# A softmax maximum added by VectorE instead of by a rank-one matmul

## The reference, cut to what matters

```python
x = x + xattn(layernorm(x), ctx)      # 8 heads of 64: q = x@Wq, k = ctx@Wk, v = ctx@Wv
                                      # softmax(q k^T / 8) v, then @Wo + bo
x = x + attn(layernorm(x))            # one head of 512, causal mask, softmax
x = x + ffn(layernorm(x))             # 512 -> 2048 -> 512, relu, values rounded to fp8 and fp16
```

## Time and profile before

| | us |
|---|---|
| three runs | 1062.31, 1063.66, 1063.72 (median 1063.66) |
| the profiled execution | 1063.23, its span 1061.4 |
| TensorE busy | 1023.5 |
| VectorE, ScalarE, GpSimd busy | 517.4, 518.4, 412.7 |
| mean granted TensorE clock | 0.991 |

### The profile page before, as it was taken

How to read it: one execution, slowest core, us unless ns; L and a number is a source line. 1 busy time by engine, 2 the same in 40 slices (tenths; PEclk the granted TensorE clock), 3 DMA queues, 4 the chain that set the end, 5 groups by cost and what they waited for, 6 DMA issues and landing times.

```text
span 1061.4 us, 23899 instructions
## 1 busy us (share of the span) xinstructions
PE 1023.5 (96%) x10317; PEld 670.8 (63%) x10320; DVE 517.4 (49%) x864; ACT 518.4 (49%) x719; POOL 412.7 (39%) x230
## 2 busy tenths in 40 slices
PE   4899999999999999999999999999998899999998
PEld 2466767677776776767677676777766544554443
DVE  6454444444444444444444444446665463564533
ACT  3345655556655565655656555565554321222220
POOL 4235454444555444454454545443344651110000
PEclk9999999999999999999999999999999899999999
DMA  7221010001011110101011100101102101012302
GB/s 267 60 90 61 31 31 31 31 31 32 31 31 44 49 31 32 31 31 31 32 31 33 57 34 31 31 31 41 45 18 81 40 1 40 2 31 90 90 30 79
DMA packets 25462, 48.98 MB, mean 46 GB/s; under 512 B 2192, under 2 KB 2192, under 8 KB 25360
## 3 DMA queue, kind: packets, MB, share of 16 engines
q1 hardware_dynamic: 24784, 46.42, 13.5%
q10 hardware_dynamic: 576, 1.05, 0.3%
HBM read 45.36 MB, written 2.10 MB: 45 GB/s over the span
## 4 chain that ended last, share of the span: by engine, by line
PE 92%; DVE 4%; DMA 1%; issue 1%; ACT 1%; POOL 1%; SPq 0%; POOLq 0%
PE v_ps L360 25%; PE k_ps L360 24%; PE e_ps L426 8%; PE c_ps L360 8%; PE e_ps L360 6%; PE o_ps L444 6%; PE c_ps L399 4%; PE o_ps L446 3%; PE e_ps L419 3%; PE m_ps L617 1%; PE o_ps L617 1%; DMA wq_raw<-in_xwq 1%; PE k_ps L538 1%; PE v_ps L590 1%; DVE stats L1011 0%
## 5 line engine op out<-in xcount | busy, mean ns | idle before, releaser
L1198 POOL TENSOR_TENSOR p_l<-p_f,p_h 128x1024 f16<-128x1024 f32 x128 | 272.4, 2128 | 407.2 <-ACT p_f L745 407.2
L742 ACT ACTIVATE p_h<-e_ps 128x1024 f16<-128x1024 f32 x128 | 131.0, 1023 | 171.8 <-PE e_ps L426 171.8
L901 DVE TENSOR_TENSOR v<-v_ps,v 128x512 f16<-128x512 f32 x128 | 88.8, 694 | 257.6 <-ACT v L726 257.6
L914 DVE TENSOR_REDUCE part_max<-c_ps 128x2 f32<-128x1024 f32 x128 | 155.7, 1217 | 0.0
L909 DVE TENSOR_TENSOR k_l<-k_ps,k_h 128x512 f16<-128x512 f32 x128 | 88.5, 691 | 113.4 <-ACT k_h L734 113.4
L734 ACT ACTIVATE k_h<-k_ps 128x512 f16<-128x512 f32 x128 | 76.4, 597 | 130.5 <-PE k_ps L360 130.5
L745 ACT ACTIVATE p_f<-e_ps 128x1024 f32<-128x1024 f32 x128 | 130.4, 1019 | 0.0
L360 PE MATMUL v_ps<-wv_h,ctx_h 128*128 128x256 f16 x768 | 127.0, 274 | 1.4 <-DVE q_l L896 1.4
L360 PE MATMUL v_ps<-wv_l,ctx_h 128*128 128x256 f16 x768 | 125.7, 273 | 0.0
L360 PE MATMUL v_ps<-wv_h,ctx_l 128*128 128x256 f16 x768 | 125.7, 273 | 0.0
L444 PE MATMUL o_ps<-v,p_h 128*128 128x130 f16 x1024 | 106.9, 221 | 7.1 <-DVE o_all L939 3.7
(11 more groups left out here) (202 smaller groups left out, 1420.3 us busy)
## 6 DMA issues: line engine op xcount, KB each, us to landing
raw<-in_ctx_t SPq DMA_DIRECT2D x32, 768.0 KB, 4.5
w_raw<-in_w_t SPq DMA_DIRECT2D x32, 256.0 KB, 2.8
xr<-in_x SPq DMA_DIRECT2D x8, 256.0 KB, 5.3
out<-xr SPq DMA_DIRECT2D x8, 256.0 KB, 2.0
x_in<-in_x ACTq DMA_DIRECT2D x4, 256.0 KB, 5.5
x_in<-in_x SPq DMA_DIRECT2D x4, 256.0 KB, 5.2
wq_raw<-in_xwq SPq DMA_DIRECT2D x1, 1024.0 KB, 9.4
raw<-in_xwo SPq DMA_DIRECT2D x4, 256.0 KB, 3.3
```

Of the source, the lines that this page charges most:

```text
L742: act.activation(p_h[:, s % P_RING, :, :, :], scores, ACT.Exp, scale=EXP_SCALE, bias=SHIFT).then_inc(p_hi, 1)
L901: dve.tensor_tensor(v[g][:, j0:j0 + 2, :, DH + 1:2 * DH + 1], v_ps[:, :].rearrange("p (j h d) -> p j h d", j=2, d=DH), v[g][:, j0:j0 + 2, ...
L914: dve.tensor_reduce(part_max[:, s % QUARTERS, :], c_ps[:, :, :], AX, ALU.max).then_inc(c_maxed, 1)
L1198: pool.tensor_tensor(p_l[:, s % P_RING, :, :, :], p_f[:, s % F_RING, :, :, :], p_h[:, s % P_RING, :, :, :], ALU.subtract).then_inc(p_split, 1)
```

## The change

The rank-one products go. The maximum is spread once a stage: VectorE multiplies the identity by the negated maximum of each head (two 128x128 bf16 products, m_diag), TensorE multiplies a matrix of ones by m_diag (256 columns, in place of the transpose), and VectorE copies the result, the same in all partitions, to m_wide (f32, two buffers). In each slot a new VectorE operation, shift, adds e_ps and m_wide into p_f, first in its queue. ScalarE's two exponentials read p_f, the second in place. scores(s) no longer waits for the copied maximum, and waits for shifted instead of p_full. The setup of `pick` on GpSimd goes.

```diff
@@ -61,7 +61,7 @@
         ("bq_col", [P, DCH], F32), ("bk_col", [P, DCH], F32), ("b1_col", [P, HC, 1], F32),
         ("b2_half", [P, D], F16),
         ("stats", [P, B, 6], F32), ("mean_var", [P, B, 2], F32), ("rstd", [P, B], F32), ("exponent", [P, B], F32),
-        ("pick", [P, P], BF16), ("m_col", [P, 2, DH], F32), ("m_row", [P, 1, T], BF16),
+        ("ones", [P, P], BF16), ("m_col", [P, 2, 1], F32), ("m_diag", [P, 2, T], BF16), ("m_wide", [P, 2, 2, 1, T], F32),
         ("part_max", [P, QUARTERS, 2], F32), ("o_rec", [P, 2, 1], F32), ("o_low", [P, 2, DH], F32),
     ])
     queries, ctx0_base = place(nc, q_base, [("q_h", [P, PAIRS, B * T], F16), ("q_l", [P, PAIRS, B * T], F16)])
...
@@ -400,31 +402,28 @@
                                    start=True, stop=True)
                 mm.then_inc(c_filled, 1)
-            def turn_maximum(n):
-                pe.wait_ge(m_ready, n + 1)
+            def spread_maximum(n):
+                pe.wait_ge(diag_ready, n + 1)
                 if n:
                     pe.wait_ge(m_copied, n)
-                pe.transpose(m_ps[:, 0:T], m_col[:, :, :].rearrange("p h d -> p (h d)"), ident[:, :]).then_inc(m_turned, 1)
+                pe.matmul(m_ps[:, 0:2 * T], ones[:, :], m_diag[:, :, :].rearrange("p h i -> p (h i)"),
+                          start=True, stop=True).then_inc(m_spread, 1)
             def scores(s):
                 n, q = stage_of(s)
                 b, p = pair_of(n)
-                pe.wait_ge(m_copied, n + 1)
                 pe.wait_ge(k_split, s + 1)
                 if s:
-                    pe.wait_ge(p_full, s)
+                    pe.wait_ge(shifted, s)
                 tokens = slice(b * T, b * T + T)
-                for h, rows in enumerate(head_rows):
-                    pe.matmul(e_ps[:, h, :].rearrange("p (j i) -> p j i", j=JT), pick[rows, :],
-                              m_row[rows, :, :].broadcast_to([DH, JT, T]), start=True, stop=False)
                 for j in range(JT):
                     keys_at = slice(q * QW + j * P, q * QW + j * P + P)
                     last = j == JT - 1
-                    for left, right, stop in ((k_h, q_h, False), (k_h, q_l, False), (k_l, q_h, last)):
+                    for left, right, first, stop in ((k_h, q_h, j == 0, False), (k_h, q_l, False, False), (k_l, q_h, False, last)):
                         for h, rows in enumerate(head_rows):
                             mm = pe.matmul(e_ps[:, h, j * T:j * T + T], left[rows, n % 2, keys_at], right[rows, p, tokens],
-                                           start=False, stop=stop)
+                                           start=first, stop=stop)
                 mm.then_inc(e_filled, 1)
             def weighted_values(s):
...
@@ -547,7 +546,7 @@
                 elif r in (2, 3, 4, 5):
                     pe.wait_ge(x1_ready, r - 1)
                 elif r == 6:
-                    pe.wait_ge(p_full, SLOTS)
+                    pe.wait_ge(shifted, SLOTS)
                 rows = slice(r * P, r * P + P)
                 three_passes(out_bank(r), (lambda c: ot_h[:, c, rows], lambda c: ot_l[:, c, rows]),
                              (lambda c: w_h[0][:, c, :], lambda c: w_l[0][:, c, :]), DCH).then_inc(acc_filled, 1)
...
@@ -735,14 +734,12 @@
             def exps(s):
-                act.wait_ge(e_filled, s + 1)
+                act.wait_ge(shifted, s + 1)
                 if s >= P_RING:
                     act.wait_ge(pv_done, s - P_RING + 1)
-                scores = e_ps[:, :, :].rearrange("p h (j i) -> p h j i", j=JT)
+                scores = p_f[:, s % F_RING, :, :, :]
                 act.activation(p_h[:, s % P_RING, :, :, :], scores, ACT.Exp, scale=EXP_SCALE, bias=SHIFT).then_inc(p_hi, 1)
-                if s >= F_RING:
-                    act.wait_ge(p_split, s - F_RING + 1)
-                act.activation(p_f[:, s % F_RING, :, :, :], scores, ACT.Exp, scale=EXP_SCALE, bias=SHIFT).then_inc(p_full, 1)
+                act.activation(scores, scores, ACT.Exp, scale=EXP_SCALE, bias=SHIFT).then_inc(p_full, 1)
             def o_lower(n):
...
@@ -916,16 +913,29 @@
             def row_maximum(n):
                 dve.wait_ge(c_maxed, 4 * n + 4)
+                dve.tensor_reduce(m_col[:, :, :], part_max[:, :, :].rearrange("p q h -> p h q"), AX, ALU.max,
+                                  negate=True).then_inc(m_ready, 1)
+
+                dve.wait_ge(m_ready, n + 1)
                 if n:
-                    dve.wait_ge(m_turned, n)
-                else:
-                    dve.wait_ge(const_ready, 6)
-                dve.tensor_reduce(m_col[:, :, 0:1], part_max[:, :, :].rearrange("p q h -> p h q"), AX, ALU.max,
-                                  negate=True).then_inc(m_ready, 1)
+                    dve.wait_ge(m_spread, n)
+                for h in range(2):
+                    ins = dve.tensor_scalar(m_diag[:, h, :], ident[:, :], m_col[:, h, :], None, ALU.mult)
+                ins.then_inc(diag_ready, 1)
             def maximum_copy(n):
-                dve.wait_ge(m_turned, n + 1)
-                dve.tensor_copy(m_row[:, 0, :], m_ps[:, 0:T]).then_inc(m_copied, 1)
+                dve.wait_ge(m_spread, n + 1)
+                dve.tensor_copy(m_wide[:, n % 2, :, 0, :], m_ps[:, 0:2 * T].rearrange("p (h i) -> p h i", h=2)).then_inc(m_copied, 1)
+
+            def shift(s):
+
+                n, q = stage_of(s)
+                dve.wait_ge(m_copied, n + 1)
+                dve.wait_ge(e_filled, s + 1)
+                if s >= F_RING:
+                    dve.wait_ge(p_split, s - F_RING + 1)
+                dve.tensor_tensor(p_f[:, s % F_RING, :, :, :], e_ps[:, :, :].rearrange("p h (j i) -> p h j i", j=JT),
+                                  m_wide[:, n % 2, :, :, :].broadcast_to([P, 2, JT, T]), ALU.add).then_inc(shifted, 1)
             def o_reciprocal(n):
                 dve.wait_ge(pv_done, 4 * n + 4)
...
@@ -977,6 +987,8 @@
             def steady(s):
                 n, q = stage_of(s)
+                if 0 <= s - E_LAG - 1 < SLOTS:
+                    shift(s - E_LAG - 1)
                 if 0 <= s - C_LAG - 1 < SLOTS:
                     quarter_maximum(s - C_LAG - 1)
                 if s >= M_LAG and (s - M_LAG) % QUARTERS == 0 and s - M_LAG < SLOTS:
...
@@ -1166,14 +1178,9 @@
             pool.affine_select(out=causal[:, :], in_=causal[:, :], compare_op=ALU.is_ge, fill=MASKED,
                                base=0, pattern=[[1, P]], channel_multiplier=-1).then_inc(const_ready, 1)
-            pool.memset(m_col[:, :, :], 0.0).then_inc(const_ready, 1)
+            pool.memset(ones[:, :], 1.0).then_inc(const_ready, 1)
             pool.memset(v[0][:, :, :, DH:DH + 1], 1.0).then_inc(v_ones, 1)
             pool.memset(v[0][:, :, :, VW - 1:VW], 0.0).then_inc(v_ones, 1)
-
-            pool.wait_ge(const_ready, 4)
-            pool.tensor_scalar(pick[:, :], ident[:, 0:1].broadcast_to([P, P]), 1.0, None, ALU.mult).then_inc(const_ready, 1)
-            pool.wait_ge(const_ready, 7)
-            pool.tensor_tensor(pick[:, :], pick[:, :], ident[:, DH:DH + 1].broadcast_to([P, P]), ALU.add).then_inc(const_ready, 1)
             def inverse_root(var, root, power, i):
```

More of the change, by code:

```diff
@@ L119, in perceiver_kernel @@
     (o_all, ident, causal, bo_row, bv_row, b2_row, bq_col, bk_col, b1_col, b2_half, stats, mean_var, rstd, exponent,
-     pick, m_col, m_row, part_max, o_rec, o_low) = keep.values()
+     ones, m_col, m_diag, m_wide, part_max, o_rec, o_low) = keep.values()
     q_h, q_l = queries.values()
@@ L195, in perceiver_kernel @@
         m_ready = sem("m_ready")
-        m_turned = sem("m_turned")
+        diag_ready = sem("diag_ready")
+        m_spread = sem("m_spread")
         m_copied = sem("m_copied")
         e_filled = sem("e_filled")
+        shifted = sem("shifted")
         p_hi = sem("p_hi")
@@ L482, in q_tile @@
                               lambda c: xt_l[:, c, half * 512:half * 512 + 512]), DCH).then_inc(q_filled, 1)
-            pe.wait_ge(const_ready, 5)
+            pe.wait_ge(const_ready, 6)
             for r in range(4):
@@ L505, in steady @@
                 if s >= M_LAG and (s - M_LAG) % QUARTERS == 0 and s - M_LAG < SLOTS:
-                    turn_maximum((s - M_LAG) // QUARTERS)
+                    spread_maximum((s - M_LAG) // QUARTERS)
                 if 0 <= s - PV_LAG < SLOTS:
```

## The result

| | before | after |
|---|---|---|
| median of 4 runs each, us | 1063.32 | 1109.23 |
| profiled execution, its span | 1063.23, 1061.4 | 1108.85, 1107.0 |
| mean granted clock | 0.991 | 0.980 |

The ratio is 1.043, 95% interval 1.0412 to 1.0448: 4.3% slower. The first part of the page, against the earlier trace rows: TensorE is 17 us less busy, VectorE 163 us more.

A forecast was written before the change was run, and what follows sets the result against it. The prediction took TensorE, busy 96% of the span, as the bound. Its terms were 1063.2 - 26.4 (pairs) + 39.3 (fourth slots) + 6.4 (last stages) + 13.6 (behind the loop) + 6 (clock) = 1102 us, range 1082 to 1134.

The forecast's parts named there:

- The saving on TensorE: In the loop, 123 slots each lose a pair of rank-one products at 0.215 us: 26.4 us saved.
- The spread maximum: Once a stage, the transpose's successor costs TensorE the same: between 0 and +0.1 us a stage, 0 taken.
- The add 1.22, the exponentials +0.03 each: In each slot, VectorE's new add takes 1.22 us and each exponential, now reading SBUF, 0.03 us more.
- The wait of the fourth slot, +1.31: Once a stage, weighted values start 1.31 us later behind o_norm: 30 slots, 39.3 us lost.
- The last four stages, +6.4 and the clock: Slots 112 to 127, which also split a late weight, lose 4 x 1.6 = 6.4 us; clock counted apart.
- the clock as a term of its own: In the last four stages and the end, 3.5 falls of TensorE's clock: +6 us.
- the round: Slots 112 to 127: VectorE's and ScalarE's steps from shift to split take 5.94 us, over the slot of 5.70.
- Behind the loop, +13.6: Slots 128 to 134: the add joins a queue that waits for others, 13.6 us lost.
- The sum: Whole kernel: 1063.2 - 26.4 + 39.3 + 6.4 + 13.6 + 6 = 1102 us.
- The clock in normal stages: Ordinary stages of the loop: TensorE idles 1.4 us, a length that leaves the granted clock at 1.00.
- The rival with 14%: In the loop, the clock falls in most stages, 1.7 us each, +30 us, 1132 us in all; chance 14%.
- The faster rival: Fourth slot's wait costs less than the pairs save: 1060 us with a 0.68 add, 1037 if hidden; chance 6%.

The follow-up runs named there:

- e3: The kernel before without the rank-one products, the maximum left out of the exponent: 1034.83 us, ratio 0.9744.
- e1: The changed kernel with o_reciprocal before the add, o_norm right behind it, and ScalarE's o_lower before the exponentials: 1054.21 us, ratio to before 0.9925.
- e7: The changed kernel with the add on half of the columns, for measuring only: 1077.94 us, ratio to before 1.0154.
- e4: The changed kernel with the add moved one slot forward behind the loop, ahead of the residual: 1093.82 us, ratio to before 1.0291.
- e5: The changed kernel with the late weight's split moved from behind k_low to behind the quarter maximum: 1101.14 us, ratio to before 1.0367.
- e9: e6 with the late weight's split left behind k_low in the second slot of a stage: 1029.31 us, ratio to before 0.9691.
- e2: The kernel before with o_reciprocal first, o_norm behind the quarter maximum, and o_lower before the exponentials: 1053.37 us, ratio 0.9914.
- e6: The changed kernel with the three reorderings of e1, e4 and e5 together: 1033.66 us, ratio to before 0.9724.

## Why the prediction was right

The forecast was 1102, the median 1109; its steps held as follows.

*The saving on TensorE*: 0.215 a pair predicted, 0.217 by e3. Right. The spread maximum costs what the transpose did (5.81 against 5.70). Right.

*The add 1.22, the exponentials +0.03 each*: 1.222, and +0.034 and +0.022. Right in the main. The 0.043 of the Trainium skill ("VectorE: DVE Perf Modes", the section on the TRN2 errata) is a little above both.

*The wait of the fourth slot, +1.31*: the slot went from 6.19 to 7.35, that is 1.16 more with 0.22 saved, +1.38. Nearly all of the 0.07 is VectorE's start 0.16 into the slot, not 0.10. e1 shows that this wait is the order's doing, and e7 that it follows the add's length one to one. In the first 112 slots: predicted 26 x 1.31 - 107 x 0.215 = +11.1, measured 12.8.

*The last four stages, +6.4 and the clock*: with the pairs and the common wait, 6.4 + 4 x 1.31 - 16 x 0.215 = 8.2, measured 16.2. The prediction had the clock as a term of its own, so the difference is the clock and the round. Of falls of the clock I expected three and a half in the whole and got four around these waits alone. Three last 3.4 us, and 4.3 us of the fourth lie in slot 127: 14.5 us at half the clock, which cost about half of that, 7, where TensorE is fully busy as in the stretches shown (an estimate: 1.1 us of the fourth lie in the wait itself). That leaves about 1 us for the round. It was 5.94 predicted, 6.45 measured, since I left out that k_low waits for v_low (0.15) and that the weight's copy is held until GpSimd's p_low ends (0.83 instead of 0.42).

*Behind the loop, +13.6*: measured 17.0, with the clock at half for some 23 us there instead of 10 (granted 0.50 in the first of these stretches of after, below). e4 takes 16 of the 17 away by order alone, and 13 us at half the clock with them, so the mechanism holds. How the 17 divide between the clock and the chain was not taken apart.

```profile
833.50:843.80 10.30, 8.01 (x91) 6.88 (x92) 4.94 (x8) 2.68 (x4) 3.60 (x3) 0.50 0.60 201
```

*The sum.* The profiled execution is 1108.9 where the sum has 1102. The first 112 slots are 1.7 over it, the last 16 are 8.0 over, the stretch behind the loop 3.4 over, and 0.5 is gained elsewhere; against these 12.6 stand the 6 that were set aside for the clock. So the term that was too small is the clock: the falls in the last 16 slots alone cost about 7, and behind the loop it was at half for 13 us more than before. I took three and a half falls of 1.7; the kernel before had one twice as long, at half from 831.2 to 838.1 around its wait of 3.71.

*The clock in normal stages* stayed at 1.00 through the 26 waits of 1.5 us (n = 1 to 26). The rival with 14% is refuted for this length; at 3.2 us the clock fell in each of the last four stages, and in e5, where the waits there were 1.9, it did not. But in e7, where they were 1.8, it fell behind the fourth of them, so at 1.8 to 1.9 us the length of the wait alone does not decide it; what else does was not tested. The rule of the Trainium skill ("TensorE: Matmul & The Clock Gate", the section on HAM oscillation), that gaps which recur can bring the gate down each time, is seen in the last four stages and not in the others. Its price, half of the slow time, is also what the shown rows give: three value products in 0.62 us at the lower level and in 0.34 at the higher.

*The faster rival* needed a shorter add, which 1.222 refutes; and where the add was as short (0.69 in e7) the stage came out at the length of before, not 0.09 below, with the last 16 slots and the stretch behind the loop longer, 1.5% slower in all.

## What to carry to other kernels

Before moving work from the bound engine to an idle one, find the chain that ends last in each stage and ask whether the new instruction enters it: here 0.88 us saved a stage met 1.38 us of latency, on an engine that was half idle. Then look at what else stands in that engine's queue; three changes of order, with no instruction removed, turned 4.3% slower into 2.8% faster, and 3.1% once one of them was refined (e9). Of this 0.9% (e2) is to be had without the change. The places to look are the stage's end, the stages with extra work, and the drain behind the loop, where an in-order queue puts early work behind late waits.

## What the runs showed of the hardware that was not expected

A VectorE operation with two SBUF operands that starts 0.03 to 0.04 us behind GpSimd's p_low waits for it: 2.64 us instead of 0.69, eight times (the second slots of the last four stages in e5 and in e6), and gone in e9, where the split starts elsewhere. The weight's copy, from f32 to f16 with one operand, waits as well: in the changed kernel, e1, e4, e7 and e9, 49 copies start while p_low runs, between 0.2 and 0.55 us before its end, and each of them ends 0.28 to 0.29 us after p_low does, whatever its start. Its 0.47 to 0.83 instead of 0.42 is therefore a wait and not a slower rate, and the 0.41 us that it adds to the round of the last 16 slots looks like the same effect as the 2.64 of e5: both end a fixed time after p_low.

The other way round GpSimd pays, and less. In the fourth slots of the last four stages, in e6 and in e9, the split's second operation starts 0.30 ahead of p_low and takes its 0.69, and p_low takes 2.38 instead of 2.13 (e9, VectorE's row and GpSimd's):

```profile
702.94 0.69 DVE L961 SCALAR_TENSOR_TENSOR wo_l<-raw,wo_h 128x512 f16<-128x512 f32 x1
```
```profile
703.24 2.38 POOL L1209 TENSOR_TENSOR p_l<-p_f,p_h 128x1024 f16<-128x1024 f32 x1 [2.92 <-ACT p_f L742]
```

Operations that read PSUM (v_low at 742.25, beside p_low from 741.87) kept their 0.69. Why the two engines collide was not taken apart.
